# Attention products with the rests of the exponentials: five units behind their scores, four buffers of rests, one sum of the last column

## The reference, cut to what matters

```python
scores = jnp.einsum('bihd,bjhd->bhij', q, k) * scale + bias   # causal
attn = jax.nn.softmax(scores, axis=-1)
y = jnp.einsum('bhij,bjhd->bihd', attn, v).reshape(B, T, H * D)
```

## Time and profile before

| | us |
|---|---|
| median of 3 runs | 3267.87 |
| lowest and highest run | 3264.66, 3268.54 |
| the profiled execution | 3262.58 |
| its span, first to last instruction | 3260.8 |
| PE busy in the span | 3085.9 |
| DVE / ACT / POOL busy | 1837.6 / 1839.4 / 1561.4 |
| mean granted TensorE clock | 0.986 of full speed |

### The profile page before, as it was taken

One profiled execution on the slowest core, in us unless ns is written; L12 is line 12 of the kernel. 1 busy time (PEld: TensorE's weight loads), 2 busy tenths in 40 slices (PEclk: granted clock), 3 DMA queues, 4 the chain that ended last, 5 costly groups with the idle time before them and its releaser, 6 DMA issues. The chain is left out here.

```text
span 3260.8 us, 46767 instructions
## 1 busy us (share of the span) xinstructions
PE 3085.9 (95%) x15184; PEld 2404.4 (74%) x15184; DVE 1837.6 (56%) x4186; ACT 1839.4 (56%) x3185; POOL 1561.4 (48%) x1359
## 2 busy tenths in 40 slices
PE   4899999999999999999999999989999999999998
PEld 3767767767767677677676776678888888788887
DVE  7676677676666766776766767553333332332323
ACT  1677777777776777777777767743333332322222
POOL 5576676676665766766766666613212220000000
PEclk7999999999999999999999999989999999999999
DMA  2342332432432424324324326244434443121210
GB/s 79 71 107 50 86 79 55 105 70 66 103 83 71 98 50 94 74 59 105 70 66 105 69 65 158 70 123 137 121 91 120 116 116 116 57 78 39 71 47 20
DMA packets 210355, 273.95 MB, mean 84 GB/s; under 512 B 68992, under 2 KB 96768, under 8 KB 209984
## 3 DMA queue, kind: packets, MB, share of 16 engines
q1 hardware_dynamic: 210112, 270.97, 32.1%
HBM read 97.25 MB, written 55.90 MB: 47 GB/s over the span
## 5 line engine op out<-in xcount | busy, mean ns | idle before, releaser
L501 POOL TENSOR_TENSOR e_lo<-e_all,e_hi 128x512 fp32r<-128x512 f32 (+1 forms) x832 | 1032.6, 1249 | 612.5 <-ACT e_all L792 526.6
L792 ACT ACTIVATE e_all<-ps_s,bias 128x512 f32<-128x512 f32 (+3 forms) x1280 | 785.3, 624 | 170.7 <-PE ps_s L1134 92.4
L785 ACT ACTIVATE e_hi<-ps_s,bias 128x512 fp32r<-128x512 f32 (+1 forms) x832 | 561.3, 675 | 203.3 <-PE ps_s L1132 125.5
L998 DVE TENSOR_REDUCE maxes<-ps_m 128x1 f32<-128x512 f32 x768 | 516.2, 685 | 225.0 <-PE ps_m L1112 222.7
L1112 PE MATMUL ps_m<-k_ext,q_max 128*128 128x512 f32 (+3 forms) x1280 | 456.2, 379 | 57.7 <-DVE maxes L995 19.5
L1131 PE MATMUL ps_s<-q_twice,k_split 128*128 128x512 f32 (+3 forms) x1280 | 484.3, 378 | 21.3 <-ACT e_all L792 19.8
L1132 PE MATMUL ps_s<-q_ext,k_ext 128*128 128x512 f32 (+3 forms) x1280 | 469.0, 366 | 0.0
L1173 PE MATMUL ps_v<-e_lo,v_both 128*65 128x512 f32 (+1 forms) x832 | 431.4, 519 | 21.0 <-POOL e_lo L501 21.0
L1112 PEld LDWEIGHTS ps_m<-k_ext,q_max 128*128 128x128 f32 x1280 | 243.0, 190 | 219.8 <-DVE maxes L995 58.9
L995 DVE CUSTOM_DVE_ANT_0 ps_m<-ps_m,mask_row 128x128 f32<-128x128 f32 (+3 forms) x512 | 252.7, 495 | 231.0 <-PE ps_m L1112 229.3
L1152 PE MATMUL ps_v<-e_all,v_full 128*65 128x512 f32 (+2 forms) x896 | 324.0, 443 | 0.0
(11 more groups left out here) (234 smaller groups left out, 6566.9 us busy)
## 6 DMA issues: line engine op xcount, KB each, us to landing
q_twice<-q_max SPq DMA_DIRECT2D x256, 128.0 KB, 2.3
yt<-y_out SPq DMA_DIRECT2D x128, 130.0 KB
k_ext<-kq_hi SPq DMA_DIRECT2D x128, 128.0 KB, 2.3
q_max<-kq_hi SPq DMA_DIRECT2D x128, 128.0 KB, 2.4
k_split<-kq_hi SPq DMA_DIRECT2D x128, 128.0 KB, 2.4
k_split<-kq_lo SPq DMA_DIRECT2D x128, 128.0 KB, 2.4
q_ext<-kq_lo SPq DMA_DIRECT2D x128, 128.0 KB, 2.4
hidden<-gelu SPq DMA_DIRECT2D x64, 256.0 KB, 2.1
```

The costliest lines, as they stand in the source:

```text
L501: on.tensor_tensor(e_lo[:, i % LO_RING, off:QB], e_all[:, u_ % E_RING, off:QB], e_hi[:, i % HI_RING, off:QB].bitcast(F32), ALU.subtract).t ...
L785: nc.scalar.activation(e_hi[:, i % HI_RING, off:QB], ps_s[u_ % 2][:, off:QB], ACT.Exp, bias=by).then_inc(hi_done, 1)
L792: nc.scalar.activation(e_all[:, u_ % E_RING, off:QB], ps_s[u_ % 2][:, off:QB], ACT.Exp, bias=by).then_inc(ex_done, 1)
L998: nc.vector.tensor_reduce(maxes[:, qt, kc:kc + 1], ps_m[m % 2][:, 0:width], AX.X, ALU.max).then_inc(mx_free, 1)
```

## The change

Three constants and what depends on them are changed. `LAG_LO` goes from 4 to 5, so a product with a rest stands one step later in PE's program. "take" is tied to `LAG_LO`, and so stands one step later too, on ACT and SP, as do "sums" and "sums out" which come with it (DVE's `RECIPROCAL`, line 1046). `e_lo` has four buffers instead of three. To make room, `last_rest` (DVE's finished sum of the last column) has one buffer instead of two, and DVE's write waits for the last product of the block before, not of the one before that. POOL's program is the same, line for line. Nothing that is computed changes, and no instruction is added or removed.

```diff
-LAG, LAG_LO = 2, 4
+LAG, LAG_LO = 2, 5
...
-E_RING, HI_RING, LO_RING, Q_RING = 3, 4, 3, 3
+E_RING, HI_RING, LO_RING, Q_RING = 3, 4, 4, 3
...
-        last = u - LAG
+        last = u + 2 - LAG_LO
         if last >= 0 and last < HEADS * NU:
...
-        last_rest = [sb(f"last_rest{i}", [P, QB], F32R) for i in range(2)]
+        last_rest = sb("last_rest", [P, QB], F32R)
...
-                            if grp >= 2:
-                                dve.wait_ge(pv_hi, units_before(*divmod(grp - 2, NQB)))
-                            nc.vector.scalar_tensor_tensor(last_rest[grp % 2][:], e_in, v_last, ps_r[:], ALU.mult, ALU.add).then_inc(rest_part, 1)
+                            dve.wait_ge(pv_hi, units_before(*divmod(grp - 1, NQB)))
+                            nc.vector.scalar_tensor_tensor(last_rest[:], e_in, v_last, ps_r[:], ALU.mult, ALU.add).then_inc(rest_part, 1)
...
-                            nc.tensor.matmul(bank[0:D, :], to_last[:], last_rest[grp % 2][:], start=False, stop=False, skip_group_check=True)
+                            nc.tensor.matmul(bank[0:D, :], to_last[:], last_rest[:], start=False, stop=False, skip_group_check=True)
```

## The result

The changed kernel takes **3290.16 us** (median of 4 runs, 3289.21 to 3295.44), the kernel before 3268.2 us beside it: a ratio of 1.0071 (95% interval 1.0053 to 1.0088), so it is slower by 22 us where 25 were forecast. The profiled execution has a span of 3288.6 us against 3260.8.

What follows compares the result with a forecast made beforehand. PE was taken to bound the kernel (3085.9 of 3260.8 us busy); 0.0 + 15.0 + 7.5 + 3.2 - 1.0 + 0.3 = +25.0 us gave 3287.6 profiled, with 5.3 added 3293 us; range 3274 to 3303.

Steps and rivals of the forecast that it cites:

- Term A: PE's 14 waits for POOL's rest (line 1173): nothing won, 0.0 us (-3 to +1); scores wait for `e_all` instead.
- Term B: POOL's copy of the values into `v_both` comes 1.0 us later, 15 times, delaying PE: +15.0 us (0 to 20).
- Term C: `y_out` directly before the third `kq_hi` delays PE's product at 618.08 by 0.5 us, 15 times: +7.5 us (0 to 9).
- Term D: One product more on PE before DVE's norms and gates, 0.23 us, 14 times: +3.2 us (0 to 3.2).
- Term E: First pair: `y_out` behind a `kq_hi`, PE's product of 97.45 comes 0.5 us earlier, again a block later: -1.0 us.

Runs made afterwards that it cites:

- the run that undoes it: Changed kernel with the copy of an odd head's values into `v_both` one rest later on POOL: 1.0039, 10.5 us under the changed kernel.
- The control: Kernel before with the copy of an odd head's values one rest later on POOL: 0.9994.
- the best version: Changed kernel with four buffers of `e_all`, three of `q_twice`, room from small tables, and the values' copy one rest later: 3259.53 us, 0.9980.

## Why the prediction was right

The time, 3290.16 us, lies 2.8 us under the forecast, and the steps held one by one. How near the median came is partly luck. The profiled execution took 3290.43 us where 3287.6 had been worked out for it, and the 5.3 us that the prediction added from that execution to the median did not show this time: the two misses run against each other. The terms are therefore held against the trace. The prediction's "own range" of 3286 to 3300 can't be worked out from the ends that it names: C and D at nothing and half of B are 18 us down, 4 up.

- **Term A** (0.0, the wait changes its name): shown by the waits of the changed kernel, where 1.69 us of the scores stand for 1.50 us of the rest product, and by the runs with four `e_all`. That the 14 waits fell to 0.36 us there shows that the reading "nothing is won because the next ring holds" named the true cause. The prediction said 1.6 us; 1.69 was measured.
- **Term B** (+15.0): 15.1 us in the first stretches of the run that undoes it (10.5 by the ratios), +1.01 us in the rows above, at the copy and at PE's product, where 1.0 was worked out. The wait of POOL was to grow to 37 us; it is 36.6 in 14. The control shows that the copy's place alone is free.
- **Term C** (+7.5): 6.75 us by the first stretches of the run with the take alone, 0.46 us at a place where 0.5 was forecast.
- **What B and C leave of the first stretch**, 3.5 of 25.3 us: by the rows it is the product that term A owes. The product with d0's rest stood at 605.86, ahead of the turn's product with `last_rest` at 607.05, where the sixth stretch ends and the first begins; now it stands behind it (612.51 behind 612.14). That moves 0.22 us in each pair from the sixth stretch to the first. The sixth is not shorter by it in the sum, since single waits there differ by up to 1.6 us.
- **Term D** (+3.2): 0.21 to 0.24 us in each of 14 pairs, 0.23 forecast. That the surplus product is the cause was argued, not tested apart; but it is in every run with the distance of five and in none with four (in the run with `q_twice` later that stretch holds other waits too).
- **Term E** (-1.0): the product of the earlier trace rows comes 0.81 us earlier, at 96.64, where 0.5 was forecast, and the first pair is 1.6 us shorter.
- **The pair** was to grow from 126.1 to 127.8 us; from 611.63 to the same wait at 739.78 it is 128.15, more by the waits for single copies by DMA, which differ from pair to pair. The stretches of 15 pairs add up to 28.9 us, with the first pair to 27.3; the profiled spans differ by 27.8 and the medians by 22 (the ratio's interval is 17 to 29 us).

The rule of the Trainium skill that the prediction set against the rows (Perfetto Trace Analysis, Optimization Strategy: the same gap repeating on the engine to be saturated can mean that there isn't room for the next tile) comes out half right. Room for the rests themselves, which this change gave, gained nothing (1.0001 with `LO_RING` at 4). But room in the ring one step up, `e_all`, closed the gap once the distance was there (1.69 to 0.36 us) and gained 30 us on the changed kernel, 19 beside the later copy. The row that names the releaser said in which ring. Against the kernel before it gained 7 us, and as much without the distance: a gap closed is not yet time won.

## What to carry to other kernels

To move a consumer further back, list every ring that its operand's producers hold while they wait, and deepen the one whose next writer would be the next to stand; the trace shows it as an equal idle of another engine that the same instruction ends. Moving a product also moves all who wait for it or for its count: here a copy on POOL into a buffer that the moved product still reads cost 15 us, more than half of the loss, and one row further back in the queue it was nearly free. Try the deeper ring on the kernel before by itself: here it gave all that the best version gave. A gain measured beside another defect isn't additive to that defect's cure: work out what each leaves at the place itself.

## What the runs showed of the hardware

- An idle of PE can cost more than itself, and the same idle does not always. Behind the wait of 2.00 us in the run with the take yet a step later the granted clock fell to half, for some 3 us, in 10 of 15 pairs and stayed at 1.00 in 5 (the waits of the ten were 1.99 to 2.00 us and one of 1.69, those of the five 1.99 to 2.12); a fall made the stretch 1.3 us longer. Behind 1.61 to 1.64 us in the middle of the odd head it fell in 7 of 13 pairs, behind 2.20 us there in 7 of 13, behind 1.50 us at the turn (kernel before) and 1.69 us (changed kernel) in none of 14. In the run with four `e_all` it fell at 710.5, inside the wait of 2.72 us, and stayed low until 717.4. So neither the length of the wait nor its place in the program decides alone; what does was not looked into. One wait of 2.00 us cost as much as two of 1.57 and 0.50 where the clock stayed, and 1.3 us more where it fell.
- A releaser is inferred, and can change its name. In the changed kernel the profile names ACT's `e_all` for POOL's wait ahead of `v_both` (36.6 us), where it named PE's product before (22.2 us). In the program the copy doesn't wait for ACT. It began at 614.39, 0.58 us after the start of PE's product with the last rest at 613.81, and 0.57 or 0.58 us after it in all 15 pairs; in the kernel before the two stood 0.65 us apart, in all 15 too.
- The queue of SP is a cost of its own. In the run with four `e_all` the copy `k_ext<-kq_hi` was issued 2.35 us later than in the changed kernel (706.50 against 704.15). Of that 0.90 us stood already ahead of the pair of `q_twice` (702.08 against 701.18); the other 1.45 came behind it, and 1.17 of them were the issue of the pair itself.
